# A recommender tower on one core: nine, two and two tables chosen by matmul instead of eight, three and three, and a feature buffer laid out slot by slot

## What is computed

```python
e = jnp.stack([tbl_0[ids[:, 0]], ..., tbl_25[ids[:, 25]]], axis=1)   # 512 x 26 x 128
T = jnp.concatenate([r_dense[:, None, :], e], axis=1)                # 512 x 27 x 128
Z = jnp.einsum('bnd,bmd->bnm', T, T)                                 # every pair's product
z = Z[:, iu0, iu1]                                                   # the 351 pairs n < m
h = jnp.concatenate([z, r_dense], axis=1)                            # 512 x 479
h = jnp.maximum(h @ W_top1 + b_top1, 0.0)                            # 512 x 512
h = jnp.maximum(h @ W_top2 + b_top2, 0.0)                            # 512 x 256
y = h @ W_top3                                                       # 512 x 1
```

## Time and profile before

| what | value |
|---|---|
| median of 3 runs | 107.55 us (106.47 to 108.98) |
| the profiled execution's own time | 107.91 us |
| its span in the profile | 106.1 us |
| instructions | 3613 |
| bytes read from HBM | 13.09 MB |

### The profile page before, as it was taken

The page is one execution under the profiler, slowest core; times in us unless marked ns, Lnnn a source line. Parts: engine busy times, 40 slices in busy tenths (PEclk is TensorE's granted clock), DMA queues, the critical chain, the costliest instruction groups (busy, mean ns, idle before and its releaser), DMA issues.

```text
span 106.1 us, 3613 instructions
## 1 busy us (share of the span) xinstructions
PE 96.3 (91%) x1499; PEld 81.3 (77%) x1499; DVE 73.0 (69%) x193; ACT 56.9 (54%) x90; POOL 59.6 (56%) x65
## 2 busy tenths in 40 slices
PE   4996799999999999999889999999599986999990
PEld 3663588888888788978688789998489964987970
DVE  5998999999999999997999553294060224016222
ACT  4847869599895997565696510046024450133020
POOL 4777777777777787777777777777740000000000
PEclk9999999999999999999999999999999999999999
DMA  2899997899959979998512222122220000000000
GB/s 55 240 273 218 243 275 157 234 268 260 272 113 271 302 141 263 276 233 238 122 43 56 56 49 56 49 66 59 54 56 6 0 6 0 6 0 0 7 0 0
DMA packets 6052, 13.32 MB, mean 126 GB/s; under 512 B 1826, under 2 KB 2595, under 8 KB 6036
## 3 DMA queue, kind: packets, MB, share of 16 engines
q1 hardware_dynamic: 4184, 9.33, 33.0%
q0 software_dynamic: 1824, 3.74, 15.3%
q10 hardware_dynamic: 28, 0.03, 0.2%
HBM read 13.09 MB, written 0.00 MB: 123 GB/s over the span
## 4 chain that ended last, share of the span: by engine, by line
PE 80%; DVE 8%; issue 6%; ACT 2%; DMA 2%; DVEq 0%
PE ps_turned L688 19%; PE ps_turned L689 19%; PE ps_prod L713 11%; PE ps_turned L659 6%; PE ps_low L746 5%; PE ps_high L746 5%; PE ps_low L754 4%; DVE sb_one_hot L509 4%; PE ps_prod L796 2%; DMA sb_ids_rows<-in_ids_chosen 2%; DVE sb_one_hot L496 1%; PE ps_pack L733 1%; PE ps_turned L782 1%; ACT sb_feats L315 1%; PE ps_turned L646 1%
## 5 line engine op out<-in xcount | busy, mean ns | idle before, releaser
L460 POOL DMA_INDIRECT sb_rows<-in_tbl,sb_ids x57 | 58.4, 1024 | 18.2 <-issue 17.1
L509 DVE TENSOR_SCALAR sb_one_hot<-sb_id_less_8p 125x512 fp32r<-125x512 f32 (+2 forms) x110 | 38.1, 401 | 1.6 <-ACT sb_id_less_8p L597 1.0
L688 PE MATMUL ps_turned<-sb_one_hot,sb_table_hi 125*128 125x512 f32 (+2 forms) x104 | 37.4, 368 | 0.6 <-DVE sb_table_lo L486 0.6
L689 PE MATMUL ps_turned<-sb_one_hot,sb_table_lo 125*128 125x512 f32 (+2 forms) x104 | 36.0, 354 | 0.0
L688 PEld LDWEIGHTS ps_turned<-sb_one_hot,sb_table_hi 125*128 125x128 f32 x104 | 19.6, 189 | 3.6 <-DVE sb_table_lo L486 1.0
L689 PEld LDWEIGHTS ps_turned<-sb_one_hot,sb_table_lo 125*128 125x128 f32 x104 | 19.7, 189 | 1.9
L486 DVE TENSOR_TENSOR sb_table_lo<-sb_table,sb_table_hi 125x512 fp32r<-125x512 f32 x28 | 18.4, 681 | 1.3 <-ACT sb_table_hi L587 1.2
L587 ACT CAST sb_table_hi<-sb_table 125x1024 fp32r<-125x1024 f32 (+1 forms) x15 | 15.2, 1012 | 4.7 <-DMA sb_table<-in_tbl 4.7
L713 PE MATMUL ps_prod<-sb_feats 128*28 128x26 f32 x1024 | 13.7, 192 | 3.2 <-issue 2.4
L713 PEld LDWEIGHTS ps_prod<-sb_feats 128*28 128x28 f32 x1024 | 11.1, 105 | 7.0 <-issue 4.4
L323 ACT COPY sb_feats<-ps_turned 128x512 f32<-128x512 f32 (+2 forms) x12 | 12.9, 1079 | 6.5 <-PE ps_turned L689 6.5
(11 more groups left out here) (89 smaller groups left out, 92.8 us busy)
## 6 DMA issues: line engine op xcount, KB each, us to landing
sb_table<-in_tbl SPq DMA_DIRECT2D x13, 448.0 KB
sb_w<-in_W_top SPq DMA_DIRECT2D x6, 256.0 KB
sb_rows<-in_tbl,sb_ids POOLq DMA_INDIRECT x57, 4.1
sb_table<-in_tbl SPq DMA_DIRECT2D x13, 52.0 KB
sb_table<-in_tbl SPq DMA_DIRECT2D x2, 224.0 KB
sb_dense_t<-in_dense_laid SPq DMA_DIRECT2D x1, 256.0 KB, 5.2
sb_w<-in_W_top SPq DMA_DIRECT2D x1, 128.0 KB
sb_b<-in_b_top SPq DMA_DIRECT2D x1, 128.0 KB
```

The costliest lines, as they stand in the source:

```text
L460: pool.indirect_dma_start(rows_of(t, s), None, tables[f], bass.IndirectOffsetOnAxis(ids_sb[:, t, f:f + 1], 0)).then_inc(rows_in[t, q], 16)
L509: dve.tensor_scalar(one_hot[:, at % ONE_HOTS, 0:width(j)], id_less_8p[:, j % NEAR, 0:width(j)], float(c), None, ALU.is_equal).then_inc(one ...
L688: pe.matmul(turned_ps[:, i % BANKS, 0:w], table_hi[:, j % SPLITS, c, :], hot, start=(c == 0), stop=False)
L689: pe.matmul(turned_ps[:, i % BANKS, 0:w], table_lo[:, j % SPLITS, c, :], hot, start=False, stop=(c == CHUNKS - 1)).then_inc(one_hot_used, 1)
```

## The change

Nine tables are chosen for all four tiles, two from tile 1 and two from tile 2: 13 tables in place of 14, with 17 + 15 + 13 + 13 = 58 gathers. The list of steps is another one that fits this arrangement. In `feats` each tile's 28 slots lie one after the other, each with its 128 samples side by side. The copies into it write runs of 128 floats or more where they wrote single floats 28 apart. The matmuls of the products read floats that lie 128 apart (512 bytes) where they read adjacent ones. Number and shape of these matmuls stay.

```diff
-CHOSEN_FROM = {0: 8, 1: 3, 2: 3}
+CHOSEN_FROM = {0: 9, 1: 2, 2: 2}
...
-P P P P G1d N0 Oa G2d H0.0 N1 P S0.0 J0 L0.0 C0.0 N2 S0.1 H0.1 J1 H0.2 G4a C0.1 L0.1 H0.3 S1 C0.2
-H1.0 N3 J2 H1.1 J3 N4 C0.3 L1.0 S2 L1.1 C1.0 H1.2 E0a C1.1 L2.0 H1.3 C1.2 S3 H2.0 C1.3 H2.1 J4
...
-X0.0 L9.1 C8.2 L10.0 C8.3 L10.1 T1.1 E8a H9.1 C9.0 H9.2 J10 X0.1 H9.3 X0.2 S11 X0.3 H10.0 C9.1
-H10.1 E1.1a C9.2 T1.2 C9.3 E1.2d X0.4 E9a X0.5 N11 H10.2 X0.6 X0.7 J11 H10.3 N12 T1.3 L11.0 J12
...
-X1.7 A0.1 V1.0 E12d H13.1 C13.0 V1.1 R0.1 C13.1 Q1.2d R0.0 T2.2 H13.2 Q1.0a H13.3 C13.2 E2.1a
-Q1.1d C13.3 E2.2d B0.0 E13a X2.0 X2.1 X2.2 X2.3 K1 B0.1 W1a T3.0 U0 X2.4 E3.0d Y0 T3.1 X2.5 E3.1a
-X2.6 A1.0 A1.1 R1.0 X2.7 R1.1 V2.0 T3.2 B1.0 Q2.0d E3.2a V2.1 Q2.1a X3.0 Q2.2a X3.1 K2 B1.1 X3.2
-U1 W2d X3.3 Y1 X3.4 X3.5 A2.0 A2.1 R2.0 X3.6 R2.1 X3.7 V3.0 B2.0 V3.1 B2.1 Q3.1a Q3.2d Q3.0d k0 U2
-f w0a k1 k2 M w1d w2a Y2 m0 m1 m2 r0a r1d r2a r3d b y
+P P P P G3a N0 Oa H0.0 N1 P S0.0 J0 H0.1 J1 C0.0 N2 L0.0 S0.1 H0.2 C0.1 G4d L0.1 H0.3 N3 S1 C0.2
+H1.0 J2 C0.3 H1.1 H1.2 S2 L1.0 E0a L1.1 C1.0 H1.3 J3 N4 H2.0 T0.0 G2a C1.1 H2.1 L2.0 N5 J4 C1.2
...
+C8.2 H9.3 C8.3 T1.1 E8a T1.2 E1.1d N10 J10 N11 X0.0 L9.0 S10 X0.1 X0.2 L9.1 X0.3 S11 C9.0 H10.0
...
+E1.0d E10a L11.1 A0.1 R0.0 S12 T2.0 L12.0 X1.0 L12.1 C11.0 H12.0 C11.1 H12.1 C11.2 E2.0d X1.1 X1.2
+X1.3 H12.2 X1.4 T2.2 C11.3 E2.2d C12.0 E11a X1.5 X1.6 R0.1 X1.7 T2.3 T2.1 V1.0 C12.1 H12.3 Q1.0a
+C12.2 E2.3d V1.1 C12.3 B0.0 Q1.2a Q1.1d E2.1a E12d K1 B0.1 W1d X2.0 U0 T3.0 X2.1 X2.2 A1.0 X2.3
+R1.0 X2.4 X2.5 E3.0a X2.6 A1.1 X2.7 R1.1 T3.1 V2.0 B1.0 V2.1 Q2.0a Q2.1a Q2.2d B1.1 E3.1d U1 Y0
+T3.2 E3.2a T3.3 K2 E3.3d W2a X3.0 X3.1 A2.0 X3.2 R2.0 X3.3 X3.4 A2.1 X3.5 R2.1 X3.6 X3.7 B2.0 V3.0
+V3.1 B2.1 Q3.0a Q3.2a Q3.1d f U2 k0 k1 k2 w0d M Y1 w1d m0 w2d Y2 m1 m2 r0a r1d r2a r3d b y
...
@@ -125,7 +124,6 @@
     NCH = len(chosen)
     CR = tables[chosen[0]].shape[0] // ROWS_PER_PART
     CHUNKS = ROWS_PER_PART
-    LEN = P * SLOTS
     HOT_PARTS, CHOOSE_PARTS, PRODUCT_PARTS, LAYER2_PARTS, LOW_PARTS = 4, 4, 8, 2, 2
 
     FIRST_PARTS = 2
@@ -192,7 +190,7 @@
         table_lo = sb("table_lo", [CR, SPLITS, CHUNKS, D], F32R)
         id_less_8p = sb("id_less_8p", [CR, NEAR, B])
         one_hot = sb("one_hot", [CR, ONE_HOTS, B], F32R)
-        feats = sb("feats", [P, TILES, LEN])
+        feats = sb("feats", [P, TILES, SLOTS, P])
         spread = sb("spread", [P, NF, QUAD])
         packed = sb("packed", [P, PK * P])
         pairs = sb("pairs", [P, 2, PK, P])
@@ -303,7 +301,7 @@
                 list(one.ap[0]), [1, b - a], [0, P]]))
 
         def feats_of(t):
-            return feats[:, t, :].rearrange("p (b s) -> p s b", s=SLOTS)
+            return feats[:, t, :, :]
 
         def empty(copy, wait, n, done_sem):
             bank = turned_ps[:, items.index(n) % BANKS, :]
@@ -319,7 +317,7 @@
                 slot = NF - 1 - j
 
                 wait(one_hot_used, CHUNKS * (j + 1))
-                dst = feats[:, start[j]:TILES, :].rearrange("p t (b s) -> p t b s", s=SLOTS)[:, :, :, slot]
+                dst = feats[:, start[j]:TILES, slot, :]
                 done = copy(dst, bank[:, 0:width(j)].rearrange("p (t b) -> p t b", b=P))
             done.then_inc(done_sem, 1)
 
@@ -374,7 +372,7 @@
             if name == "blanks":
                 k, = n
                 blank = [prod_ps[:, 0:QUAD // 2, 0:NF - 1], prod_ps[:, QUAD // 2:QUAD, 0:NF - 1],
-                         feats[:, :, :].rearrange("p t (b s) -> p (t b) s", s=SLOTS)[:, :, NF:SLOTS],
+                         feats[:, :, NF, :],
                          packed[:, NP:PK * P], spread[:, NF - 1:NF, :]][k]
 
                 wait(zeros_ready, 1)
@@ -383,7 +381,7 @@
                      ).then_inc(blanks_ready, 1)
             if name == "dense":
                 wait(dense_in, 16)
-                copy(feats[:, :, :].rearrange("p t (b s) -> p t b s", s=SLOTS)[:, :, :, 0],
+                copy(feats[:, :, 0, :],
                      dense_t[:, :].rearrange("p (t b) -> p t b", b=P)).then_inc(dense_ready, 1)
             if name == "empty":
                 empty(copy, wait, n, emptied[me])
@@ -709,9 +707,9 @@
                             pe.wait_ge(spread_ready, 2 * t)
                     for i in range(part * QUAD // PRODUCT_PARTS, (part + 1) * QUAD // PRODUCT_PARTS):
                         for quad in range(P // QUAD):
-                            at = (quad * QUAD + i) * SLOTS
+                            b = quad * QUAD + i
                             done = pe.matmul(prod_ps[quad * QUAD:quad * QUAD + SLOTS, i, 0:NF - 1],
-                                             feats[:, t, at:at + SLOTS], feats[:, t, at:at + NF - 1],
+                                             feats[:, t, :, b], feats[:, t, 0:NF - 1, b],
                                              start=True, stop=True)
                     if part == PRODUCT_PARTS - 1:
                         done.then_inc(prods_ready, 1)
```

More of the change, by code:

```diff
@@ L49 @@
 ORDER = """
-P P P P G1d N0 Oa G2d H0.0 N1 P S0.0 J0 L0.0 C0.0 N2 S0.1 H0.1 J1 H0.2 G4a C0.1 L0.1 H0.3 S1 C0.2
-H1.0 N3 J2 H1.1 J3 N4 C0.3 L1.0 S2 L1.1 C1.0 H1.2 E0a C1.1 L2.0 H1.3 C1.2 S3 H2.0 C1.3 H2.1 J4
-T0.0 H2.2 E1a C2.0 L2.1 H2.3 C2.1 L3.0 C2.2 H3.0 S4 H3.1 N5 N6 E0.0a C2.3 L3.1 L4.0 C3.0 E2a H3.2
-C3.1 H3.3 G3a J5 H4.0 C3.2 Da H4.1 T0.1 L4.1 C3.3 S5 H4.2 C4.0 H4.3 G0a E3a L5.0 C4.1 H5.0 C4.2
-E0.1a H5.1 H5.2 T0.3 J6 L5.1 C4.3 E0.3a H5.3 C5.0 H6.0 S6 N7 N8 C5.1 J7 L6.0 E4a L6.1 C5.2 H6.1
@@ L55 @@
-C5.3 H6.2 T0.2 H6.3 E5a C6.0 H7.0 J8 H7.1 N9 C6.1 S7 T0.4 C6.2 E0.2a L7.0 H7.2 C6.3 S8 L7.1 N10
-C7.0 H7.3 E6a H8.0 C7.1 E0.4a H8.1 C7.2 S9 L8.0 L8.1 C7.3 J9 H8.2 H8.3 C8.0 E7a L9.0 C8.1 H9.0 S10
-X0.0 L9.1 C8.2 L10.0 C8.3 L10.1 T1.1 E8a H9.1 C9.0 H9.2 J10 X0.1 H9.3 X0.2 S11 X0.3 H10.0 C9.1
-H10.1 E1.1a C9.2 T1.2 C9.3 E1.2d X0.4 E9a X0.5 N11 H10.2 X0.6 X0.7 J11 H10.3 N12 T1.3 L11.0 J12
-T1.0 S12 L11.1 C10.0 V0.0 C10.1 E1.3a H11.0 H11.1 C10.2 E1.0a V0.1 C10.3 H11.2 Q0.1a H11.3 L12.0
-E10a L12.1 T2.0 H12.0 C11.0 H12.1 E2.0a X1.0 H12.2 X1.1 X1.2 Q0.0d S13 C11.1 C11.2 L13.0 C11.3
@@ L61 @@
-L13.1 C12.0 E11d X1.3 H12.3 X1.4 N13 Q0.2d C12.1 J13 X1.5 T2.1 H13.0 K0 C12.2 W0d C12.3 A0.0 X1.6
-X1.7 A0.1 V1.0 E12d H13.1 C13.0 V1.1 R0.1 C13.1 Q1.2d R0.0 T2.2 H13.2 Q1.0a H13.3 C13.2 E2.1a
-Q1.1d C13.3 E2.2d B0.0 E13a X2.0 X2.1 X2.2 X2.3 K1 B0.1 W1a T3.0 U0 X2.4 E3.0d Y0 T3.1 X2.5 E3.1a
-X2.6 A1.0 A1.1 R1.0 X2.7 R1.1 V2.0 T3.2 B1.0 Q2.0d E3.2a V2.1 Q2.1a X3.0 Q2.2a X3.1 K2 B1.1 X3.2
-U1 W2d X3.3 Y1 X3.4 X3.5 A2.0 A2.1 R2.0 X3.6 R2.1 X3.7 V3.0 B2.0 V3.1 B2.1 Q3.1a Q3.2d Q3.0d k0 U2
-f w0a k1 k2 M w1d w2a Y2 m0 m1 m2 r0a r1d r2a r3d b y
+P P P P G3a N0 Oa H0.0 N1 P S0.0 J0 H0.1 J1 C0.0 N2 L0.0 S0.1 H0.2 C0.1 G4d L0.1 H0.3 N3 S1 C0.2
@@ new lines @@
+H1.0 J2 C0.3 H1.1 H1.2 S2 L1.0 E0a L1.1 C1.0 H1.3 J3 N4 H2.0 T0.0 G2a C1.1 H2.1 L2.0 N5 J4 C1.2
+H2.2 E0.0a H2.3 C1.3 L2.1 S3 N6 C2.0 H3.0 J5 H3.1 C2.1 E1a H3.2 C2.2 L3.0 S4 L3.1 C2.3 L4.0 N7
+C3.0 H3.3 H4.0 S5 C3.1 L4.1 C3.2 J6 H4.1 E2a H4.2 C3.3 H4.3 Da C4.0 L5.0 H5.0 N8 E3a C4.1 H5.1
+C4.2 S6 H5.2 L5.1 T0.1 C4.3 H5.3 E0.1a H6.0 C5.0 E4a H6.1 C5.1 L6.0 J7 H6.2 T0.2 J8 C5.2 L6.1 G1a
+H6.3 C5.3 S7 C6.0 E0.2a L7.0 C6.1 H7.0 S8 H7.1 C6.2 E5a L7.1 C6.3 H7.2 N9 L8.0 T0.3 E6a H7.3 C7.0
+L8.1 G0a T0.4 C7.1 H8.0 E0.3a H8.1 C7.2 E0.4a H8.2 J9 C7.3 H8.3 C8.0 H9.0 E7a H9.1 C8.1 H9.2 S9
@@ new lines @@
+C8.2 H9.3 C8.3 T1.1 E8a T1.2 E1.1d N10 J10 N11 X0.0 L9.0 S10 X0.1 X0.2 L9.1 X0.3 S11 C9.0 H10.0
+L10.0 C9.1 J11 H10.1 E1.2a C9.2 H10.2 X0.4 L10.1 X0.5 X0.6 X0.7 C9.3 V0.0 N12 V0.1 C10.0 E9a Q0.2d
+C10.1 J12 H10.3 Q0.1d C10.2 Q0.0d H11.0 K0 L11.0 C10.3 W0a H11.1 T1.3 H11.2 T1.0 H11.3 E1.3a A0.0
+E1.0d E10a L11.1 A0.1 R0.0 S12 T2.0 L12.0 X1.0 L12.1 C11.0 H12.0 C11.1 H12.1 C11.2 E2.0d X1.1 X1.2
+X1.3 H12.2 X1.4 T2.2 C11.3 E2.2d C12.0 E11a X1.5 X1.6 R0.1 X1.7 T2.3 T2.1 V1.0 C12.1 H12.3 Q1.0a
+C12.2 E2.3d V1.1 C12.3 B0.0 Q1.2a Q1.1d E2.1a E12d K1 B0.1 W1d X2.0 U0 T3.0 X2.1 X2.2 A1.0 X2.3
```

## The result

The changed kernel took 119.9 us against 108.19 us for the kernel before (medians of four each). Some executions of a kernel run over 1.5% longer than its fastest, most of them at a lower granted clock; the ratios and their intervals leave these out, and here they give 1.110, 95% interval 1.086 to 1.134. The profiled execution took 121.0 us with a mean granted clock of 0.986; the two executions at a clock of 1.00 took 118.74 and 118.80 us.

What follows compares the result with a forecast made beforehand. TensorE was taken as the bound, with VectorE loaded beside it until about 70 us. Arrangement and copies (-0.8 + 0.2 - 0.8 = -1.4 us) plus products (+4.8) gave +3.4 us: 111.0 us from 107.55, range 105.0 to 121.5.

Steps and rivals of the forecast that it cites:

- The case taken: Whole kernel: strided product reads take TensorE twice as long, 111.0 us, chance 0.37.
- What bounds the kernel: TensorE and VectorE loaded together up to about 70 us, then TensorE alone; an added TensorE microsecond lengthens the kernel equally.
- The products: Product matmuls on TensorE, reading with a stride: slower by +4.8 us, bounded between no change and +55 us.
- TensorE doubles: 1024 product instructions at 15.4 ns instead of 7.7: +7.2 us, less 2.4 us of vanishing "issue" waits, +4.8 us.
- The factor of ScalarE's copies: Copies into the feature buffer: steps of 28 floats take 1.9 times the contiguous time on ScalarE, applied to TensorE's reads.
- the quads stop overlapping: Rival for the products: reads 512 bytes apart not served side by side, 22.6 ns each, +10.7 us, 118.3 us, chance 0.21.
- Free read: Rival for the products: the strided read costs TensorE nothing, leaving 105 to 107 us, chance 0.32.
- The copies: Contiguous copies into the feature buffer spare TensorE waits: -0.8 us on the path, bounds -0.3 to -1.6.
- The arrangement: Nine, two and two tables: -0.8 us of TensorE work, +0.2 us for VectorE while it is full.
- The gathers: POOL's chain of gathers, one more than before, the 58th: costs 0 us.
- Just in time: The 58th gather lands at 82.8 us, 84.5 at worst; its transpose stands at about 84 us: 0 us.

Runs made afterwards that it cites:

- the run with pairs: The kernel before with only its feature buffer reordered so two samples lie side by side (products step 8 bytes): 108.36 us against 108.97, ratio 0.984.
- the arrangement alone: The kernel before with only the 9, 2 and 2 tables and their list of steps, buffer still sample by sample: 104.74 us against 108.97, ratio 0.966.
- the version with both gains: The kernel before given 9, 2 and 2 tables and two samples side by side: ratio 0.953 in the first set of executions, 0.963 in the second.

## Why the prediction was right, and where its steps were off

*The forecast as a whole.* The direction was right, and so was its reason: slower, because the strided products take TensorE longer. The size was not. The case taken, 111.0 us with a range of its own from 108.5 to 113.5, did not come; +3.4 us were forecast and +11.7 us measured. The stated range holds 119.9 us because it takes in the rival at 118.3 us, which had 0.21, and to that extent it is luck.

*What bounds the kernel.* Right for TensorE: its products' extra time, +11.2 us, shows in the kernel's +11.7 us. Two readings were off. VectorE falls from 9 at about 58 us, not 70 (the 23rd of the 40 digits in the earlier trace rows). And POOL's gathers, priced at 0 us, are part of the path in the changed kernel up to 72.95 us.

*The products.* The sign was right, the size was not. The term was "TensorE doubles", 7.7 x 2 = 15.4 ns and +4.8 us; measured were 24.8 ns and +11.2 us. The factor of ScalarE's copies was taken as the nearest row. It is near what a read with each float in its own 16-byte block costs: 13.9 and 14.0 ns at 528 and 16 bytes. What the copies couldn't show is the 512: their step was 112 bytes. The rule of the Trainium skill (Advanced Engine Details and Errata, Memory Cachelines) agrees with the free step of 8 bytes, two hits to a line, and with the penalty at 16 and 528 bytes. The steep part, 15.6 to 24.8 ns at 544, 576 and 512 bytes, is what the runs add.

*The rival "the quads stop overlapping".* It gave 22.6 ns and 118.3 us, and is nearest to what came: 24.8 ns and 119.9 us. Its number was near; its mechanism has the runs against it. It counted the moving operand alone, 26 columns that would take 22.6 ns once reads 512 bytes apart no longer go side by side. With only the moving operand strided the pace was 15.0 ns, so the quads still overlapped there; 24.8 ns came only with the weights' cost on top. What in the memory makes 512 bytes so dear stays open.

*Free read.* Refuted at 512 bytes, true at 8.

*The copies.* A contiguous copy of 512 elements was put at 0.64 and 0.74 us at most and took 0.583 to 0.586 us on ScalarE. What they are worth on the path was put at -0.8 us, bounds -0.3 to -1.6; the run with pairs gave -1.7 us (-0.6 to -2.9 by its interval) at an unchanged product time. That agrees with the bounds and leaves room for more; I had counted TensorE's direct waits only.

*The arrangement.* Put at -0.8 + 0.2 us; measured -3.4%, some -3.8 us. Two terms were off. The "issue" stalls went with the list of steps (-2.1 us idle and -1.1 us busy in the products), and I had let them go only where reads become slow. In the other direction the wait of TensorE for VectorE is 2.8 instead of 0.6 us where I allowed 0.5. The rest isn't taken apart.

*The gathers.* "Just in time" was right with the adjacent reads: 0.3 us of wait in the arrangement alone, last gather at 79.35 us. In the changed kernel they were late by another cause, the stretched instructions on POOL, which no step of mine had: 1.8 us of wait, though not at the 58th gather, where I had forecast none. Whether the lower clock behind such a wait is the difference between the executions of 118.8 and of 121 to 122 us was not tested.

## What to carry to other kernels

Before turning a layout so that the writers get contiguous runs, ask at what distance the reader then steps, and for TensorE be wary of one like 512 bytes: 16 bytes of padding took the products here from 24.8 to 13.9 ns each. Better still is a layout between the two: with two samples side by side the writers had most of their gain (664 ns against 1206, and 583 fully contiguous) and the reader lost nothing. And when two things change at once, run each alone: here a gain of 3.4% was hidden in a change that lost 11%, and the products' net +11.2 us hid a cost of 14.4 us.

## What the runs showed of the hardware that was not expected

Beside matmuls that read both operands 512 bytes apart, instructions of ScalarE and VectorE last several times as long, some up to the end of the stretch of matmuls (3.40 us instead of 0.59 for one activation, 1119 ns instead of 366 on average for those of the first layer); some gathers of POOL do so too (3.54 us instead of 1.02), but none of over 1.34 us where VectorE is idle. With both operands at 528 bytes, or with adjacent floats, nothing of this is seen. With one operand at 512 bytes or both at 576 it isn't on ScalarE and VectorE, while POOL had no gathers left to show it.

The cost of TensorE's strided read is graded: 14, 15.6, 17.9 and 24.8 ns at 16 or 528, 544, 576 and 512 bytes, and the costs of the two operands add up.

In the executions with late tables TensorE's granted clock is down over long stretches. Window of the version with both gains, first set:

```profile
60.00:84.00 24.00, 6.99 (x15) 3.87 (x15) 2.03 (x4) 2.72 (x4) 13.50 (x15) 0.50 0.16 42
```

TensorE is busy for 7 of 24 us there and gets 0.50, its level of 1.2 GHz.
